# Decay rows masked by a shifted DRAM-to-DRAM transfer, GpSimd left with a power and three scatters behind the output projection

## What is computed

```python
gc = jnp.cumsum(g, axis=-1)
dec = gc[..., :, None] - gc[..., None, :]
mask = jnp.tril(jnp.ones((C, C), bool))
A = jnp.einsum('bhntd,bhnsd->bhnts', q, k)
A = A * jnp.where(mask, jnp.exp(jnp.where(mask, dec, 0.0)), 0.0)
o_intra = jnp.einsum('bhnts,bhnsd->bhntd', A, v)
...
on = o * jax.lax.rsqrt(jnp.mean(o * o, axis=-1, keepdims=True) + EPS) * gnorm_w
o = on * (g * jax.nn.sigmoid(g))
return o @ Wo
```

## Time and profile before

| what | value |
|---|---|
| median of 3 runs | 427.65 us (425.81 to 429.51) |
| profiled execution, its own time | 427.74 us |
| its span in the trace | 426.0 us |
| TensorE busy in the span | 388.3 us |
| VectorE busy | 321.0 us |
| ScalarE busy | 307.1 us |
| GpSimd busy | 283.8 us |

### The profile page before, as it was taken

The page is one execution under the profiler, slowest core; times in us unless marked ns, Lnnn a source line. Parts: engine busy times, 40 slices in busy tenths (PEclk is TensorE's granted clock), DMA queues, the critical chain, the costliest instruction groups (busy, mean ns, idle before and its releaser), DMA issues.

```text
span 426.0 us, 13509 instructions
## 1 busy us (share of the span) xinstructions
PE 388.3 (91%) x3650; PEld 336.3 (79%) x3651; DVE 321.0 (75%) x868; ACT 307.1 (72%) x947; POOL 283.8 (67%) x237
## 2 busy tenths in 40 slices
PE   7979999979989989989989899989999999999990
PEld 5657888867767777777767778889999999999990
DVE  5987888987878877877877877856766777777750
ACT  4988988777786886886877878657666766666660
POOL 6012442486887877878878863438888888888884
PEclk9998999999999999999999999999999999999996
DMA  8856485534644324545545333026554555555530
GB/s 238 216 168 218 133 306 207 165 122 138 183 125 153 132 90 134 173 121 169 156 133 166 97 109 109 27 51 72 67 69 59 74 65 65 69 64 73 65 35 0
DMA packets 59096, 51.29 MB, mean 120 GB/s; under 512 B 7200, under 2 KB 51392, under 8 KB 59072
## 3 DMA queue, kind: packets, MB, share of 16 engines
q1 hardware_dynamic: 45936, 42.07, 34.3%
q0 software_dynamic: 12272, 8.54, 14.5%
q10 hardware_dynamic: 864, 0.40, 0.4%
HBM read 33.14 MB, written 18.30 MB: 121 GB/s over the span
## 4 chain that ended last, share of the span: by engine, by line
PE 57%; issue 11%; POOL 9%; DVE 8%; ACT 8%; DMA 3%; SPq 1%; DVEq 1%; ACTq 1%; POOLq 0%
PE psA L911 15%; PE psVG L899 15%; ACT E L1079 5%; PE psVG L720 5%; POOL sorted_rows L544 4%; PE psA L736 4%; PE psQK L708 3%; DVE msn L1411 3%; PE psT L781 3%; POOL rms L538 3%; PE psO L755 3%; PE psT L789 2%; DMA x_all<-in_L_attn_x_dram 1%; SPq L343 1%; ACT sq L1088 1%
## 5 line engine op out<-in xcount | busy, mean ns | idle before, releaser
L578 POOL DMA_INDIRECT out_dram<-yw,sidx x71 | 114.6, 1615 | 29.2 <-issue 11.9
L544 POOL DMA_INDIRECT sorted_rows<-x_all,pos_i x64 | 73.0, 1140 | 35.3 <-PE psT L781 26.3
L1079 ACT ACTIVATE E<-gcB,ngc 128x128 f32<-128x128 f32 x256 | 78.5, 400 | 0.5 <-DMA gcB<-decay_rows 0.5
L531 POOL TENSOR_SCALAR_AFFINE_SELECT E<-E 128x1024 f32<-128x1024 f32 x32 | 35.3, 1102 | 63.6 <-ACT E L1079 63.3
L538 POOL TENSOR_TENSOR rms<-msn,neg_half 128x8 f32<-128x8 f32 x32 | 53.3, 1666 | 7.5 <-DVE msn L1411 6.8
L1052 ACT ACTIVATE qb<-psQK,qmask 128x256 f32<-128x256 f32 x64 | 26.9, 472 | 38.8 <-PE psQK L708 33.1
L1439 DVE TENSOR_TENSOR pr<-psA,E 128x512 f32<-128x512 f32 x64 | 41.0, 681 | 16.8 <-POOL E L531 16.7
L755 PEld LDWEIGHTS psO<-v_sb,pr 128*64 128x64 f32 x1024 | 39.0, 139 | 17.2 <-issue 12.1
L755 PE MATMUL psO<-v_sb,pr 128*64 128x64 f32 x1024 | 43.0, 226 | 7.0 <-DVE og L1451 4.6
L911 PE MATMUL psA<-xT_all,v_sb 128*128 x288 | 38.3, 276 | 0.4 <-issue 0.4
L899 PE MATMUL psVG<-xgT,gcB 128*128 128x128 f32 x288 | 38.6, 277 | 0.0
(11 more groups left out here) (197 smaller groups left out, 922.1 us busy)
## 6 DMA issues: line engine op xcount, KB each, us to landing
gcB<-decay_rows SPq DMA_DIRECT2D x32, 512.0 KB
sorted_rows<-blank SPq DMA_DIRECT2D x12, 396.0 KB, 5.2
xg<-sorted_rows SPq DMA_DIRECT2D x71, 66.0 KB
x_all<-in_L_attn_x_dram SPq DMA_DIRECT2D x16, 256.0 KB, 5.2
out_dram<-res SPq DMA_DIRECT2D x32, 128.0 KB
eqB<-decay_exp_rows SPq DMA_DIRECT2D x32, 64.0 KB
w1b<-in_L_ffn_w_dram SPq DMA_DIRECT2D x8, 256.0 KB
xT_all<-in_L_ffn_w_dram SPq DMA_DIRECT2D x32, 64.0 KB
```

The source lines that it names most:

```text
L531: nc.gpsimd.affine_select(out=E[j][:], in_=E[j][:], pattern=[[0, 2 * H], [1, P]], compare_op=ALU.is_ge, fill=0.0, base=0, channel_multipli ...
L544: nc.gpsimd.indirect_dma_start(out=sorted_dram, out_offset=bass.IndirectOffsetOnAxis(ap=pos_i[:, t:t + 1], axis=0), in_=x_all[:, t, :], in ...
L578: nc.gpsimd.indirect_dma_start(out=out_rows, out_offset=bass.IndirectOffsetOnAxis(ap=sidx[j][:], axis=0), in_=yw[j][:], in_offset=None, bo ...
L1079: last = nc.scalar.activation(E[j][:, k, h * P:(h + 1) * P], gcB[j][:, k * H + h, :], ACT.Exp, bias=ngcf[:, bass.ds((s * 2 + k) * H + h, 1)])
```

## The change

The mask moves into the data that E is made from. A decay row is stored with 128 values of -1e30 behind it (padded_dram, rows of 256). For each step from the third on, `mask_rows` copies, for each of 128 partitions p and 8 rows r, the 128 values that begin at place p of row r, so the row moved left by p with -1e30 behind, into masked_dram[j] (DRAM to DRAM, 1024 pieces of 512 B). `load_gc` reads that tensor with a pitch one element smaller than the one it was written with, so partition p starts p elements early: each row is moved back to the right by p, and what stands in front is the -1e30 of the row ahead, or of the gap that `fill_gaps` writes once. The exponential makes these places 0. Steps 0 and 1 keep the old broadcast and `mask_dec`. `mask_rows` of step s+3 is issued in step s, behind `load_gc` of s+2, which itself waits for its own masked rows.

GpSimd's step keeps `rms_step`, first in order now, and then waits for the output projection of s-2 (wo_ready) and issues all three scatters together. `probs` waits for e_ready.

```diff
+NEVER = -1e30
+GAP = 32
...
-    gc_dram = nc.dram_tensor("decay_rows", [TH, P], F32).ap()
+    gc_dram = nc.dram_tensor("decay_rows", [2 * 2 * H, P], F32).ap()
+    padded_dram = nc.dram_tensor("decay_rows_padded", [TH, 2 * P], F32)
+    masked_dram = [nc.dram_tensor(f"decay_masked{j}", [P, 2 * H * P + GAP + 1], F32) for j in range(2)]
...
-        gcT = sb("gcT", [P, 2, P])
+        gcT = sb("gcT", [P, 2, 2 * P])
...
+            def store_first_rows():
+                sp.wait_ge(act_decay, 4)
+                sp.dma_start(gc_dram, gcT[0:2 * 2 * H, 0, 0:P]).then_inc(gc_stored, 16)
+            def store_exps(a):
                 sp.wait_ge(act_decay, a * DECAY_N + 5)
                 sp.dma_start(eq_rows[:, a, :], eqT[:, a, :]).then_inc(eq_stored[a], 16)
+            def store_padded(a):
+                sp.wait_ge(act_decay, a * DECAY_N + 4)
+                sp.wait_ge(pad_made, 1)
+                sp.dma_start(padded_rows[:, a, :], gcT[:, a, :]).then_inc(padded_stored[a], 16)
+            ROW = 2 * H * P
+            def fill_gaps(j):
+                sp.dma_start(bass.AP(masked_dram[j], ROW, [[ROW + GAP + 1, P], [1, GAP + 1]]), gcT[:, 0, P:P + GAP + 1]).then_inc(dec_masked[j], 16)
+            def mask_rows(i, j):
+                s = i * 2 + j
+                sp.dma_start(masked_dram[j].ap()[:, 0:ROW].rearrange("p (r t) -> p r t", t=P),
+                             bass.AP(padded_dram, s * (2 * H * 2 * P), [[1, P], [2 * P, 2 * H], [1, P]])).then_inc(dec_masked[j], 16)
             def load_gc(i, j):
                 s = i * 2 + j
-                sp.dma_start(gcB[j][:].rearrange("p h t -> p (h t)"),
-                             gc_dram[bass.ds(s * 2 * H, 2 * H), :].rearrange("r t -> (r t)").partition_broadcast(P)).then_inc(gcB_loaded[j], 16)
+                if isinstance(i, int) and s < 2:
+                    src = gc_dram[bass.ds(s * 2 * H, 2 * H), :].rearrange("r t -> (r t)").partition_broadcast(P)
+                else:
+                    sp.wait_ge(dec_masked[j], (i + 1) * 16)
+                    src = bass.AP(masked_dram[j], 0, [[ROW + GAP, P], [1, ROW]])
+                sp.dma_start(gcB[j][:].rearrange("p h t -> p (h t)"), src).then_inc(gcB_loaded[j], 16)
...
+            store_first_rows()
+            store_exps(0)
+            sp.wait_ge(gc_stored, 16)
             load_gc(0, 0)
             sp.wait_ge(eq_stored[0], 16)
             load_eq(0, 0)
             load_gc(0, 1)
             load_eq(0, 1)
+            store_padded(0)
+            for j in range(2):
+                fill_gaps(j)
+            sp.wait_ge(padded_stored[0], 16)
+            for j in range(2):
+                mask_rows(1, j)
...
                     load_gc(i + 1, j)
+                if not (isinstance(i, int) and s == 0) and inside(i, j, 3, SEQS):
+                    i1, j1 = turn(i, j, 1, 2)
+                    sp.wait_ge(gcB_loaded[j1], (i1 + 1) * 16)
+                    mask_rows(i1 + 1, j1)
...
-            store_decays(1)
+            store_exps(1)
+            store_padded(1)
...
+            nc.gpsimd.memset(gcT[:, :, P:2 * P], NEVER).then_inc(pad_made, 1)
...
                 t = (s - PLACE_FROM) * 3
-                if s < SEQS:
-                    mask_dec(*divmod(s, 2))
-                if s == PLACE_FROM:
-                    pool.wait_ge(dve_late, LATE)
-                    pool.wait_ge(sort_cleared, CLEARS * 16)
-                if s >= PLACE_FROM and t < TILES:
-                    pool.wait_ge(qk_ready, s + 2)
-                    place_rows(t)
+                if s < 2:
+                    mask_dec(0, s)
                 if s >= 1:
                     if s >= 2:
                         pool.wait_ge(dve_on, s - 1)
                     rms_step(*divmod(s - 1, 2))
                 if s == 2:
                     finish_band()
-                if s >= PLACE_FROM and t + 1 < TILES:
-                    place_rows(t + 1)
-                    pool.wait_ge(oT_ps_ready, s)
-                    place_rows(t + 2)
+                if s == PLACE_FROM:
+                    pool.wait_ge(dve_late, LATE)
+                    pool.wait_ge(sort_cleared, CLEARS * 16)
+                if s >= PLACE_FROM and t < TILES:
+                    pool.wait_ge(wo_ready, s - 1)
+                    for k in range(3):
+                        place_rows(t + k)
...
             def probs(i, j):
                 s = i * 2 + j
-                dve.wait_ge(e_masked, s + 1)
+                if isinstance(i, int) and s < 2:
+                    dve.wait_ge(e_masked, s + 1)
+                else:
+                    dve.wait_ge(e_ready, s + 1)
```

More of the change, by code:

```diff
@@ L247, in build_layer @@
         w_loaded = sem("w_loaded")
-        gc_stored = [sem(f"gc_stored{a}") for a in range(2)]
+        gc_stored = sem("gc_stored")
+        padded_stored = [sem(f"padded_stored{a}") for a in range(2)]
+        dec_masked = [sem(f"dec_masked{j}") for j in range(2)]
+        pad_made = sem("pad_made")
         eq_stored = [sem(f"eq_stored{a}") for a in range(2)]
@@ L359, in clear @@
                 sp.dma_start(cleared[:, k:k + 1, :, :].rearrange("p a n c -> p (a n) c"), blank[:]).then_inc(sort_cleared, 16)
-            gc_rows = gc_dram.rearrange("(a p) t -> p a t", p=P)
+            padded_rows = padded_dram.ap().rearrange("(a p) t -> p a t", p=P)
             eq_rows = eq_dram.rearrange("(a p) t -> p a t", p=P)
-            def store_decays(a):
-                sp.wait_ge(act_decay, a * DECAY_N + 4)
-                sp.dma_start(gc_rows[:, a, :], gcT[:, a, :]).then_inc(gc_stored[a], 16)
+            def store_first_rows():
+                sp.wait_ge(act_decay, 4)
+                sp.dma_start(gc_dram, gcT[0:2 * 2 * H, 0, 0:P]).then_inc(gc_stored, 16)
@@ L367, in store_decays @@
+            def store_exps(a):
                 sp.wait_ge(act_decay, a * DECAY_N + 5)
                 sp.dma_start(eq_rows[:, a, :], eqT[:, a, :]).then_inc(eq_stored[a], 16)
-            store_decays(0)
-            sp.wait_ge(gc_stored[0], 16)
+            def store_padded(a):
[3 more added lines that the diff above has]
+            ROW = 2 * H * P
@@ L415, in _ @@
             step(1, 1)
-            sp.wait_ge(gc_stored[1], 16)
+            sp.wait_ge(padded_stored[1], 16)
             sp.wait_ge(eq_stored[1], 16)
@@ L439, in _ @@
                         sp.dma_start(w2_sb[:, e, c, :], w2[e, c * P:(c + 1) * P, :].rearrange("e f d -> f e d")).then_inc(w_loaded, 16)
-            with sp.Fori(SEQS // 4 + 1 + EXP // 2, SEQS // 2 - 1) as i:
+            with sp.Fori(SEQS // 4 + 1 + EXP // 2, SEQS // 2 - 2) as i:
                 for j in range(2):
                     step(i, j)
+            for j in range(2):
+                step(SEQS // 2 - 2, j)
             def load_block(i, j):
@@ L1022, in decay_rows @@
                 act.wait_ge(pe_decay, [1, 4][a])
-                nc.scalar.copy(gcT[:, a, :], psT[:, 0:P]).then_inc(act_decay, 1)
+                nc.scalar.copy(gcT[:, a, 0:P], psT[:, 0:P]).then_inc(act_decay, 1)
             def decay_exps(a):
```

## The result

The changed kernel takes 460.23 us (median of 4 runs, 457.67 to 464.38) against 426.81 us (425.81 to 429.51) of the kernel before on the same chip: ratio 1.078, interval 1.068 to 1.089. It is slower by 33 us where 18 us of gain were forecast.

A forecast was written before the change was run, and what follows sets the result against it. GpSimd's closed round was taken to bound the 22 scatter steps (7.88 us against TensorE's 6.90). At 7.05 us a step 18.2 us are won, all else 0: 427.74 - 18.2 = 409.5 us, forecast 406 to 414, full range 405.5 to 428.

The forecast's parts named there:

- The closed round of GpSimd: Scatter steps: scatter, mask, scatter, power, `on` and transposes wait on each other, 7.84 us; opening it wins 18.2 us.
- Rival (a): Loop: back-to-back scatters and VectorE hold each other up, 7.5 us a step, 419.4 us; chance 0.18, shared with mild DMA limits.
- Rival (d): GpSimd: the round closes another way, power behind scatters behind projection, 424 to 431 us; no-change chance 0.10, shared with DMA.
- The mask on GpSimd: Removing 30 of 32 masks, 1.10 us each, helps only scatter steps, as a link of the round and end of msn's wait.
- the masked rows by DMA: Loop: 512 KB more a step, 3.1 us of all engines (2.0 to 4.1), hidden within 7.05 us; cost 0.
- The masked rows are issued a further step ahead: SyncE: early issue gives lead, so a surplus of 1 us over 8 weight steps fits in 8 us; nothing waits.
- Rival (b): Loop: DMA partly bounds; at 4.8 us a transfer 429.5 us; no-change chance 0.10 shared, mild forms within 0.18.
- rival (c): Loop: DMA engines bound outright from about 5 us a transfer; 452 us at 5.5, 468 at 6.1; chance 0.14.
- Loads of gcB from distinct rows: Decay loads replacing a broadcast: same bytes to SBUF, counted at 0.
- Start-up and the two stores of padded rows: Before the loop: smaller first store wins 0 to 0.3 us; all start-up and rest taken as 0, -0.5 to +1.
- signs against it: ScalarE's E waiting for gcB, SyncE waiting for masked rows (transfer above 4 us), or msn beyond 1 us.
- signs for it: Scatter steps about 7.0 us, msn 0.2 to 0.5 us, three scatters in one run, no gcB wait, DMA share 0.75 to 1.

The follow-up runs named there:

- e1: Kernel before with the change's GpSimd order, old broadcast loads, no masked transfer, no mask from step 2 on: 405.46 us, ratio 0.951.
- e10: Changed kernel with GAP = 63 alone (masked rows written at a pitch of 4352 B, mask whole), first chip: 405.42 us, ratio 0.949.
- e11: Kernel before, GpSimd order mask, power, one scatter, wait for the projection, two scatters; no masked transfer; first chip: 406.11 us, ratio 0.950.
- e12: The changed kernel again, word for word, on the first chip: 445.91 us (437.50 to 450.85), ratio 1.043.
- e17: The changed kernel a third time, word for word, on a third chip: 443.37 us, ratio 1.039.
- e9: Changed kernel, source not shifted, written and loaded at aligned pitches, no mask from step 2 on; repeated on the first chip: 405.68 us, ratio 0.950.
- e13: Changed kernel with only the source not shifted (writes still at 4228 B), no mask from step 2 on; first chip: 444.02 us, ratio 1.040.
- e14: Changed kernel with GAP = 7, rows written at a pitch of 4128 B (multiples of 32 B): 405.84 us, ratio 0.950.
- e16: Changed kernel with GAP = 31, rows written at a pitch of 4224 B (multiples of 128 B): 406.48 us, ratio 0.950.
- e3: Changed kernel with four masked buffers in place of two, masked rows issued five steps ahead; first chip: 450.34 us, ratio 1.054.
- e18: Changed kernel with four masked buffers, masked rows issued five steps ahead, again, on a third chip: 435.14 us, ratio 1.018.
- e15: Changed kernel with GAP = 15, rows written at a pitch of 4160 B (multiples of 64 B): 406.60 us, ratio 0.952.
- e8: Kernel before, GpSimd order mask, power, one scatter, wait for the projection, two scatters; second chip: 441.99 us, ratio 1.031.
- e6: Changed kernel with GAP = 63 alone (masked rows written at a pitch of 4352 B), second chip: 452.41 us, ratio 1.063.

## Why the prediction was wrong, step by step

**The compute side was right, a little low.** The closed round of GpSimd was opened: with the transfer out of the way (e1, e10) a step is 6.89 us, against 7.05 taken and 6.90 for TensorE alone. The gain is 427.1 - 405.5 = 21.7 us where 18.2 was taken and 21.5 was the bound. msn runs 0.17 us and was not late: it begins at 212.62 in e10, while the third scatter runs, from 211.94 to 212.90 (both rows are shown in the last section). I had laid it behind the third scatter because it waited behind GpSimd's work in the earlier trace rows; here it ran during a scatter. Rival (a), scatters that disturb, did not come with this order: in e10 they take 1.03, 0.96 and 0.96 us. Rival (d) did not either.

**The mask on GpSimd** was one link of the round, but it need not go: e11 keeps all 32 and gains as much on that chip. The prediction asked what its removal frees, not whether another place is free.

**The step that failed is the term "the masked rows by DMA", taken at 0.** Three things in it, in the order of their weight:

1. The price of writes at any multiple of 4 B. The range of 2.0 to 4.1 us of the engines was right: 4.1, 3.5 and 3.5 us in the three comparisons of the changed kernel (e12: 57.8% of 435.7; e17: 57.3% of 438.0). But I took the middle, 3.1, with one word for source and target. They are not alike. A shifted source adds 0.2 us where the writes are aligned (e9 1.9, e10 2.1) and 0.4 where they are not (e13 3.1, e12 3.5), and nothing to the time. Writes at every multiple of 4 B take 3.1 to 4.1 us against 1.9 to 2.3. e10 and e14 to e16 take this one thing away and win it all back.
2. "The masked rows are issued a further step ahead" gave a lead that is not there. `load_gc` waits for its own rows and stands ahead of the next `mask_rows` in SyncE's queue, so one transfer is in flight at a time and a step is at least landing + 0.5 us: 8.3 + 0.5 = 8.8, which is the measured distance. The prediction compared a sum of engine times with the step, and had no row that compared the time to landing with it. At 3.1 us (e13) its sum says hidden, and 444 us was measured.
3. Even with the string cut (e3, e18) the sum does not hold. There the share is 1.04 and more, and a transfer takes 4.5 and 3.9 us (e18: 61.0% of 432.6, less 146.1, over 30 is 3.9). Rival (b)'s sum gives some 423 and 410 us at these values; 450 and 435 were measured. What it lacks is again a time to landing: the loads of gcB, 10 us in e18. How the fuller engines and the order of SyncE's queue share in that was not told apart.

The first time fell into rival (c), 452 to 468 us, at a chance of 0.14; the later ones, 446 and 443, lie below it. That the size fits is partly luck: (c) wanted 5 us of the engines a transfer, and 3.5 to 4.1 were enough, because the string binds first.

**Zero terms.** Loads of gcB from distinct rows land in 4.0 us (4.08 in the earlier trace rows): right. Start-up and the two stores of padded rows: e10 and e1, with and without them, differ by 0.04 us, where the runs of each scatter by 1 to 2 us: right. What the prediction named as signs against it, E waiting for gcB from decay_masked and SyncE for masked rows, is what came (71.5 us and 132.6 us), with msn not beyond 1 us. Three scatters in one run and a DMA share of 0.75 to 1, named as signs for it, came as well, so the share was no sign.

**The Trainium skill.** The runs now show what they could not before. A masked transfer with its rows written at multiples of 32 B takes 1.9 to 2.3 us of the engines. The Trainium skill (DMA: Bandwidth & Descriptors, Latency and other measured facts), by its rate for copies between HBM tensors in far longer rows, made it 2.5 us, an estimate: somewhat high. The same page of the Trainium skill (How a descriptor splits into AXI transactions) wants multiples of 256 B and made it 3.7 us, an estimate. An increase of that size is not seen for the shifted reads (e10: 2.1), nor for writes at multiples of 32, 64 or 128 B (2.3, 2.2 and 2.1). For writes at every multiple of 4 B the size is about what it says, 3.1 to 4.1 us. It spoke against this change, and I gave it no chance of its own; but at 3.7 us too my sum would have said hidden.

## What to carry to other kernels

Before a transfer is added to a loop, ask how many of its kind are in flight, and compare time to landing plus issue with the step; a DMA share below 1 answers neither. Write DRAM rows at a pitch that is a multiple of at least 32 B, the smallest that was cheap here, and put the odd shift on the reading side: one constant was worth 32 to 40 us on the first chip. And first try to move an instruction to a free place of its engine (e11) before moving it to another resource.

## What the runs showed of the hardware that was not expected

**Writes to DRAM in pieces of 512 B** took 1.9 to 2.3 us of 16 engines for 512 KB when rows began at multiples of 32 B or more, and 3.1 to 4.5 us at multiples of 4 B. With one transfer in flight, time to landing was 6.4 and 6.6 us (e10, e15) against 7.5 to 8.3 us. Reads of 512 B and 4096 B that began at any multiple of 4 B added nothing to the time of e10 and 0.2 us to its engine time.

**The same kernel on another chip.** e10's and e8/e11's kernels take 405 to 406 us on the first chip, 452 and 442 us on the second, where the kernel before took its usual 427.73. There ScalarE's square of psO waits although psO is done. e6, last matmuls of psO, third scatter and square:

```profile
202.49 0.64 PE L795 MATMUL psO<-v_sb,pr 128*64 128x64 f32 x16
...
204.94 0.96 POOL L587 DMA_INDIRECT sorted_rows<-x_all,pos_i  x1 [0.31 <-issue]
...
206.89 0.60 ACT L1128 ACTIVATE sq<-psO 128x512 f32<-128x512 f32 x1 [3.25 <-remote]
```

e10, the same three, with the second scatter and msn:

```profile
209.38 0.63 PE L795 MATMUL psO<-v_sb,pr 128*64 128x64 f32 x16
...
210.67 0.96 POOL L587 DMA_INDIRECT sorted_rows<-x_all,pos_i  x1 [0.30 <-issue]
...
211.18 0.59 ACT L1128 ACTIVATE sq<-psO 128x512 f32<-128x512 f32 x1
...
211.94 0.96 POOL L587 DMA_INDIRECT sorted_rows<-x_all,pos_i  x1 [0.30 <-issue]
...
212.62 0.17 DVE L1451 SCALAR_TENSOR_TENSOR msn<-ms,vpe 128x8 f32<-128x8 f32 x1
```

In e10 the square begins 1.2 us behind psO, while the second scatter runs; in e6 3.8 us behind it and 1.0 us behind the end of the third scatter. In the three steps of e6 from 183 to 208 that distance is 0.9 to 1.0 us, and in four steps of e8 from 180 to 209 it is 1.0 to 1.3 us. So on that chip something of ScalarE's stood behind the run of scatters; what it was, and how many chips do so, stays open. Whether e1, e10 and e11 beat the kernel before is therefore shown for the first chip only.

**The changed kernel differs between comparisons:** 460, 446 and 443 us, where the kernel before stays within 426.65 to 427.73 in all of them. So does the one with four buffers, 450 us on the first chip (e3) and 435 on the third (e18). The changed kernel's time is that of a string of DMA landings (8.3, 7.5 and 7.5 us), and what sets those 0.8 us is open too.
